# Top-2 gates of a mixture-of-heads layer: both gates in one pass, 16-bit marks, expert outside the head

## The reference

```python
gate_v = jnp.einsum('btc,hec->bthe', x, Ws)      # 16 heads, 8 experts
w, sel = jax.lax.top_k(gate_v, 2)
wsig = jax.nn.sigmoid(w)
oh = jax.nn.one_hot(sel, E, dtype=x.dtype)
mix_v = jnp.einsum('bthk,bthke->bthe', wsig, oh)  # weights of the values
...
gate_o = jnp.einsum('btc,hec->bthe', x, Wd)
_, sel_o = jax.lax.top_k(gate_o, 2)
mask_o = jax.nn.one_hot(sel_o, E, dtype=x.dtype).sum(axis=3)
```

## Time and profile before

| | us |
|---|---|
| median of 3 runs | 2720.51 |
| lowest, highest | 2718.44, 2722.49 |
| profiled execution, its own time | 2725.65 |
| span of the profiled execution | 2723.8 |
| granted TensorE clock, mean | 0.976 of 2.4 GHz |

### The profile page before, as it was taken

One profiled execution on the slowest core, in us unless ns is written; L12 is line 12 of the kernel. 1 busy time (PEld: TensorE's weight loads), 2 busy tenths in 40 slices (PEclk: granted clock), 3 DMA queues, 4 the chain that ended last, 5 costly groups with the idle time before them and its releaser, 6 DMA issues.

```text
span 2723.8 us, 51202 instructions
## 1 busy us (share of the span) xinstructions
PE 2556.2 (94%) x17437; PEld 1698.5 (62%) x17437; DVE 2135.7 (78%) x3151; ACT 1854.0 (68%) x4430; POOL 740.4 (27%) x564
## 2 busy tenths in 40 slices
PE   5699998999999999999899999999999999999997
PEld 3557675665666656566565666656566665666665
DVE  7588776989799798879987998797788879775552
ACT  3366755867688677867767877686687768766663
POOL 1000000544055125504440452264045215400000
PEclk9799999999999999999999999999999999999997
DMA  3425353664566546556573755556466564645434
GB/s 138 139 72 139 94 150 98 162 174 120 150 151 180 129 134 175 139 153 163 133 183 88 198 151 142 162 152 170 111 186 162 148 160 132 189 102 149 113 80 93
DMA packets 753406, 385.77 MB, mean 142 GB/s; under 512 B 421568, under 2 KB 678656, under 8 KB 752768
## 3 DMA queue, kind: packets, MB, share of 16 engines
q1 hardware_dynamic: 747104, 380.66, 52.5%
q10 hardware_dynamic: 6048, 1.84, 0.3%
HBM read 274.91 MB, written 115.87 MB: 143 GB/s over the span
## 4 chain that ended last, share of the span: by engine, by line
PE 65%; DVE 17%; issue 7%; DMA 4%; ACT 3%; SPq 2%; POOL 2%; ACTq 0%; DVEq 0%; POOLq 0%
PE ps L717 14%; PE ps L739 13%; PE ps L726 12%; PE ps L786 7%; PE ps L706 7%; DVE h_ring L1226 5%; PE ps L792 4%; DVE h_nmax L1048 3%; PE ps L799 2%; SPq L515 2%; DVE h_ring L1236 1%; DMA v_d<-h_v_mixed 1%; PE ps L758 1%; POOL h_ring L653 1%; PE ps L826 1%
## 5 line engine op out<-in xcount | busy, mean ns | idle before, releaser
L893 ACT ACTIVATE h_prob<-ps,h_nmax 128x512 f32<-128x512 f32 x1024 | 709.7, 695 | 96.5 <-DVE h_nmax L1048 94.6
L1048 DVE TENSOR_REDUCE h_nmax<-ps 128x2 f32<-128x1024 f32 x512 | 621.6, 1214 | 117.0 <-PE ps L717 116.0
L726 PE MATMUL ps<-ident,h_prob 128*128 128x128 f32 x4096 | 620.8, 279 | 23.4 <-DVE h_probT L1288 13.3
L726 PEld LDWEIGHTS ps<-ident,h_prob 128*128 128x128 f32 x4096 | 479.3, 144 | 193.5 <-issue 115.2
L717 PE MATMUL ps<-h_qk 64*128 64x512 f32 x2048 | 585.5, 649 | 1.4 <-ACT h_prob L893 1.2
L1013 ACT ACTIVATE h_probT<-ps 128x512 f32<-128x512 f32 x796 | 478.0, 600 | 61.7 <-PE ps L726 59.3
L662 POOL TENSOR_TENSOR h_wide_c<-h_wide_c,h_ring 128x512 f32<-128x512 f32 x240 | 333.3, 1389 | 678.6 <-DVE h_ring L1236 678.6
L739 PE MATMUL ps<-h_probT,h_v_sb 128*64 128x256 f32 x4096 | 502.4, 388 | 6.0 <-DMA h_v_sb<-v_d 4.2
L739 PEld LDWEIGHTS ps<-h_probT,h_v_sb 128*64 128x64 f32 x4096 | 273.2, 137 | 312.8 <-issue 149.5
L1226 DVE TENSOR_TENSOR_SCAN h_ring<-h_ring 128x512 f32<-128x512 f32 x256 | 406.5, 1588 | 39.3 <-POOL h_ring L653 24.9
L653 POOL TENSOR_TENSOR h_ring<-h_m_xpad,h_m_b_rows 128x512 f32<-128x512 f32 x256 | 351.0, 1381 | 263.1 <-DVE h_m_xpad L1347 251.5
(11 more groups left out here) (215 smaller groups left out, 2597.7 us busy)
## 6 DMA issues: line engine op xcount, KB each, us to landing
h_mix_diag<-mix_blocks SPq DMA_DIRECT2D x128, 512.0 KB, 4.1
v_d<-h_v_mixed SPq DMA_DIRECT2D x128, 256.0 KB, 4.3
h_v_sb<-v_d SPq DMA_DIRECT2D x128, 256.0 KB, 3.3
at_d<-h_att SPq DMA_DIRECT2D x128, 256.0 KB, 3.1
h_mo_diag<-mo_blocks SPq DMA_DIRECT2D x128, 256.0 KB, 3.5
h_att<-at_d SPq DMA_DIRECT2D x128, 256.0 KB, 3.7
h_m_b_rows<-dbl_d SPq DMA_DIRECT2D x128, 256.0 KB, 4.5
h_m_c_rows<-dbl_d SPq DMA_DIRECT2D x128, 256.0 KB, 4.5
```

Of the source, the lines that this page charges most:

```text
L726: ins = pe.transpose(ps[:, TB + v % 2, k * P:(k + 1) * P], prob[:, v % NB, k * P:(k + 1) * P], ident[:, :])
L893: act.activation(prob[:, v % NB, :], ps[:, SB + v % 4, :], ACT.Exp, bias=nmax[:, p, j, o:o + 1], accum_out=den[:, p, j, o:o + 1]).then_inc ...
L1048: dve.tensor_reduce(nmax[:, p, j, :], ps[:, SB + 2 * w % 4:SB + 2 * w % 4 + 2, :], X, ALU.max, negate=True).then_inc(sem("row_max"), 1)
```

## The change

Both gates go through `top2` together: 12 steps at prep steps 18 to 29, each over 1024 elements per partition (2 gates x 4 rows x 8 experts x 16 heads), and none at steps 45 to 56. The gates are laid out with the expert outside and the head innermost: the weights `gateT` are turned into this order once at the start, when ScalarE copies them from PSUM. So the maximum over experts runs over elements that lie 16 apart, and the mix no longer has to change the order; the marks of the output gate are turned back, in f32, by the last instruction. `key`, `pick`, `first_key` and the maximum of the keys are 16-bit whole numbers; the gates and their maximum stay f32. The first greatest gate is taken away in place in `gates`. The greatest gates lie in the memory of the layer norm's result, which has been turned by then. `mix` and the marks of the output gate have memory of their own, and the wait for the mix's DMA stands before the next job's mix. The last step has two sums of 512 elements, and the mix is one instruction. The store of the marks stays at step 57.

```diff
-        first_key = sb("first_key", [P, E])
+        first_key = sb("first_key", [P, E * H], U16)
...
-            g_top = t("g_top", [P, J * H])
-            g_key = t("g_key", [P, J * H, E])
-            g_rest = t("g_rest", [P, J, H * E])
-            chosen = t("chosen", [P, 2, J, H * E])
-            g_sig = t("g_sig", [P, J, H * E])
-            mix = g_key[:, :, :].rearrange("p (j e a) b -> p j e (a b)", j=J, e=E)
+            GATES_AT_ONCE = 2
+            g_top = nrm[:, 0, 0:GATES_AT_ONCE * J * H].rearrange("p (n h) -> p n h", h=H)
+            g_first = t("g_first", [P, GATES_AT_ONCE * J, H], U16)
+            g_key = t("g_key", [P, 2, J, E * H], U16)
+            g_pick = t("g_pick", [P, 2, J, E * H], U16)
+            chosen_o = t("chosen_o", [P, J, H * E])
+            g_sig = t("g_sig", [P, J, E * H])
+            mix = t("mix", [P, J, E * H])
...
-                                    sp.wait_ge(sem("chosen"), 2 * n + 2)
-                                    sp.dma_start(rows(mo_d[n]), chosen[:, 1, :, :]).then_inc(sem("mo_out"), 16)
+                                    sp.wait_ge(sem("chosen_o"), n + 1)
+                                    sp.dma_start(rows(mo_d[n]), chosen_o[:, :, :]).then_inc(sem("mo_out"), 16)
...
-                                act.wait_ge(sem("chosen"), 2 * n)
+                                act.wait_ge(sem("chosen_o"), n)
...
                     def top2(i, a, m):
+                        n = GATES_AT_ONCE * J
                         r, part = divmod(m, TOP_PARTS)
...
+                        g, key, pick = (z[:, a:a + GATES_AT_ONCE, :, :].rearrange("p a j (e h) -> p (a j) e h", h=H)
+                                        for z in (gates, g_key, g_pick))
+                        top, first = (z[:, :, :].rearrange("p n (o h) -> p n o h", o=1).broadcast_to([P, n, E, H])
+                                      for z in (g_top, g_first))
+                        by_expert = first_key[:, :].rearrange("p (n c) -> p n c", n=1).broadcast_to([P, n, E * H])
                         linked()
+                        if m == TOP_PARTS - 1:
+                            link(dve.scalar_tensor_tensor(
+                                out=g.rearrange("p n e h -> p (n e h)"), in0=pick.rearrange("p n e h -> p (n e h)"),
+                                scalar=NEG, in1=g.rearrange("p n e h -> p (n e h)"), op0=ALU.mult, op1=ALU.add))
+                            return
                         if part == 0:
-                            link(dve.tensor_reduce(g_top[:, :], g, X, ALU.max))
+                            link(dve.tensor_reduce(g_top[:, :, :], g.rearrange("p n e h -> p n h e"), X, ALU.max))
                         elif part == 1:
-                            if a == 1:
-                                dve.wait_ge(sem("mix_out"), 16 * (i + 1))
                             link(dve.tensor_tensor(key, g, top, ALU.is_equal))
                         elif part == 2:
-                            link(dve.tensor_tensor(key, key, fk, ALU.mult))
+                            flat = key.rearrange("p n e h -> p n (e h)")
+                            link(dve.tensor_tensor(flat, flat, by_expert, ALU.mult))
                         elif part == 3:
-                            link(dve.tensor_reduce(g_top[:, :], key, X, ALU.max))
+                            link(dve.tensor_reduce(g_first[:, :, :], key.rearrange("p n e h -> p n h e"), X, ALU.max))
                         elif part == 4:
-                            if r == 0 and a == 1 and i >= 1:
-                                dve.wait_ge(sem("mo_out"), 16 * i)
-                            link(dve.tensor_tensor(pick if r == 0 else key, key, top, ALU.is_equal))
-                        elif r == 1:
-                            dve.tensor_tensor(pick, pick, key, ALU.add).then_inc(sem("chosen"), 1)
+                            link(dve.tensor_tensor(pick if r == 0 else key, key, first, ALU.is_equal))
                         else:
...
+                            if a == 0:
+                                ins = dve.tensor_tensor(g_pick[:, 0, :, :], g_pick[:, 0, :, :], g_key[:, 0, :, :], ALU.add)
+                                ins.then_inc(sem("chosen_v"), 1)
+                            if a + GATES_AT_ONCE == 2:
+                                if i >= 1:
+                                    dve.wait_ge(sem("mo_out"), 16 * i)
+                                dve.tensor_tensor(chosen_o[:, :, :].rearrange("p j (h e) -> p j e h", e=E),
+                                                  g_pick[:, 1, :, :].rearrange("p j (e h) -> p j e h", h=H),
+                                                  g_key[:, 1, :, :].rearrange("p j (e h) -> p j e h", h=H),
+                                                  ALU.add).then_inc(sem("chosen_o"), 1)
...
                     def mix_gates(i):
...
-                        for j in range(J):
-                            ins = dve.scalar_tensor_tensor(out=mix[:, j, :, :].rearrange("p e h -> p h e"),
...
+                        if i >= 1:
+                            dve.wait_ge(sem("mix_out"), 16 * i)
+                        dve.wait_ge(sem("chosen_v"), i + 1)
+                        dve.scalar_tensor_tensor(out=mix[:, :, :], in0=g_sig[:, :, :], scalar=1.0, in1=g_pick[:, 0, :, :],
+                                                 op0=ALU.add, op1=ALU.mult).then_inc(sem("mix"), 1)
...
-                                for a in range(2):
+                                for a in range(0, 2, GATES_AT_ONCE):
                                     if TOP_AT[a] <= u < TOP_AT[a] + 2 * TOP_PARTS:
                                         top2(n, a, u - TOP_AT[a])
```

More of the change, by code:

```diff
@@ L17 @@
 U32 = mybir.dt.uint32
+U16 = mybir.dt.uint16
 ALU = mybir.AluOpType
@@ L414, in macaron_kernel @@
             turns = [(w_raw["L0_W"][:, 0, :], WkT[:, :]), (w_raw["L0_W"][:, 1, :], WvT[:, :])]
-            turns += [(w_raw["Ws"][:, 0, :], gateT[:, 0, :]), (w_raw["Wd"][:, 0, :], gateT[:, 1, :])]
+            turns += [(w_raw[name][:, 0, :], gateT[:, a, :].rearrange("p (e h) -> p e h", h=H)) for a, name in enumerate(("Ws", "Wd"))]
             turns += [(w_raw["Wv"][:, a, :], WveT[:, a * P:(a + 1) * P]) for a in range(E * DH // P)]
@@ L627, in _ @@
                                     sp.dma_start(mix_d.rearrange("(j p) c -> p j c", p=P),
-                                                 mix[:, :, :, :].rearrange("p j e h -> p j (e h)")
+                                                 mix[:, :, :]
                                                  ).then_inc(sem("mix_out"), 16)
@@ L677, in _ @@
                             for e in range(E):
-                                pool.memset(first_key[:, e:e + 1], float(E - e)).then_inc(sem("masks"), 1)
+                                pool.memset(first_key[:, e * H:(e + 1) * H], float(E - e)).then_inc(sem("masks"), 1)
                             for h in range(HALVES):
@@ L994, in _ @@
                         act.wait_ge(sem("w_turned"), n + 1)
-                        act.activation(dst, ps[:, n % 2, 0:D], ACT.Copy).then_inc(sem("w_turned_out"), 1)
+                        src = ps[:, n % 2, 0:D]
+                        if len(dst.shape) == 3:
+                            src = src.rearrange("p (h e) -> p e h", h=H)
+                        act.activation(dst, src, ACT.Copy).then_inc(sem("w_turned_out"), 1)
                     act.wait_ge(sem("w_turned_out"), len(turns))
@@ L1103, in top2 @@
-                        key = g_key[:, :, :]
-                        pick = chosen[:, a, :, :].rearrange("p j (h e) -> p (j h) e", e=E)
-                        linked()
+                        g, key, pick = (z[:, a:a + GATES_AT_ONCE, :, :].rearrange("p a j (e h) -> p (a j) e h", h=H)
+                                        for z in (gates, g_key, g_pick))
+                        top, first = (z[:, :, :].rearrange("p n (o h) -> p n o h", o=1).broadcast_to([P, n, E, H])
+                                      for z in (g_top, g_first))
@@ L1119, in top2 @@
-                            link(dve.tensor_tensor(pick if r == 0 else key, key, top, ALU.is_equal))
-                        elif r == 1:
-                            dve.tensor_tensor(pick, pick, key, ALU.add).then_inc(sem("chosen"), 1)
-                        else:
-                            link(dve.scalar_tensor_tensor(
-                                out=g_rest[:, :, :].rearrange("p j c -> p (j c)"),
-                                in0=pick.rearrange("p n e -> p (n e)"), scalar=NEG,
-                                in1=gates[:, a, :, :].rearrange("p j c -> p (j c)"), op0=ALU.mult, op1=ALU.add))
@@ L1128, in mix_gates @@
-                    def mix_gates(i):
-                        dve.wait_ge(sem("chosen"), 2 * i + 1)
-                        linked()
-                        for j in range(J):
-                            ins = dve.scalar_tensor_tensor(out=mix[:, j, :, :].rearrange("p e h -> p h e"),
```

(8 more changed lines are left out.)

## The result

The changed kernel takes 2796.76 us (median of 4 runs, 2791.96 to 2801.1) against 2719.57: a ratio of 1.0265, 95% interval 1.0245 to 1.0286, so 72 us or 2.6% slower. The forecast was slower, by 28 us. The direction came as predicted and the size at two and a half times, above the upper end of the range.

The account below looks back on a forecast made before the run. No single engine was the bound: TensorE held 65% of the chain, VectorE 17%, full in A with room in B. 39 + 7 - 12 - 4 - 2 = +28 us on 2720.5 gave 2748 us, range 2706 to 2786.

Parts of the forecast that it names:

- A: Prep steps 18 to 30, value gate's top-2 and mix: grows by 6.9 us against 1.8 us idle; 39 us together.
- First job: Its gates run before attention starts and are the chain itself, so all 6.9 us count: 7 us.
- D: A windows of jobs 4, 6, 8 and 14, where VectorE is the chain: all 24 us of surplus count.
- M: A windows of jobs 5, 10 and 11, VectorE a fifth to under half of the chain: 7 of 18 us count.
- P: The other eight A windows, VectorE next to nothing in the chain: a quarter of 34 us counts, 8 us.
- The 1.7 us between a row maximum and its exponential: Seen in A of job 12; a lag of that size was to cost nothing, the rest of 4.3 us per window in part.
- B: Steps 45 to 57, output gate's top-2: shrinks by 8.2 us; gives 12 us in jobs 1, 3, 9 and 4 elsewhere.
- The 2 us for fewer clashes with GpSimd: VectorE's two-input time per job falls from 11.9 to 8.6 us, so fewer clashes: -2 us.
- the stride was not free: Rival on the strided reduces in A: they cost nothing extra, A grows by 3.9 us, about 2725 us; chance 0.18.
- the 16-bit products and compares: Rival on A: 16-bit operations run at full length (1.2 us), A grows by 9.3 us, 2768 us; chance 0.12.
- hardly any lag was absorbed: Against the rival that score banks absorb the lag in A, giving 2708 us, or 2700 with cheap reduces; chance 0.22.
- C: Steps 31 to 44, between the two gate windows; the forecast had no term for it.

Follow-up runs that it names:

- five: Kernel before without the rule for ties, five gate instructions in place of twelve per gate; against the kernel before 0.9875, -34 us.
- the half dose: Kernel before with five added reduces of 512 elements, 3.4 us, in every second of prep steps 19 to 28; against the kernel before 1.0107, +29 us.
- a_plus10: Kernel before with ten added reduces of 512 elements, 6.8 us, one a step in prep steps 19 to 28; against the kernel before 1.0264, +72 us.
- no_b: Kernel before with the output gate's twelve top-2 instructions replaced by one copy of the value gate's marks; against the kernel before 0.9984, -4 us.

## Why the prediction missed the size

1. *Prices of the operations*: right within 0.1 us, but for the 16-bit strided reduce (2.04 for 1.89) and the turned sum (1.28 for 1.02). By the groups' busy time, with what overlap with GpSimd adds, the gates in A went from 9.9 (half of the top-2 groups, and the mix) to 16.9 us a job: 7.0 more, where 6.9 was said.
2. *First job*: 7 forecast, 8 measured, of which 1.3 lie before its gates.
3. *What the extra costs in A*: this is the step that failed. I had the surplus over the idle right, 24 + 18 + 34 = 76 us in D, M and P, and then let it count in full in D alone, four tenths in M and a quarter in P: 39 us. The windows grew by 21.6, 16.5 and 34.8: 73 us. The share of the chain that an engine holds tells what a microsecond less gives, as five shows. For a microsecond more, its idle tells more, and in P VectorE was nearly as full as in D (2.6 us idle a window against 1.0). The 1.7 us between a row maximum and its exponential I had taken as room for a lag in every window; the half dose lengthened A by 24.5 us where its surplus is 31, so such room gave back 6 or 7 us over all fifteen windows at most. One rival is left for a part of it. TensorE's granted clock fell in most of the longer windows, and its busy time in A rose from 461.62 to 476.81 us. In a_plus10 seven A windows stayed at the full clock and grew by 21.8 us for a surplus of 28; the eight at 0.88 to 0.96 grew by 45.9 for 46. So most of the loss comes without the clock, and whether the clock adds some us is open.
4. *B*: 16 forecast, 8 measured (6.4 in no_b): TensorE and SyncE's queue hold it. Of the jobs 1, 3 and 9, which were to give 12, only job 3 gave much (3.4; the others 0.9 and 0.4), and job 2 gave 3.0.
5. *SyncE's wait for the mix* (L627, now L630): it was 12.4 us after 12.5; I had said that it grows. The 2 us for fewer clashes with GpSimd can't be told apart in any run.
6. *Rivals*: the stride was not free, the 16-bit products and compares took 0.68 us and not 1.22, and hardly any lag was absorbed. All three were decided by durations and windows as named. With the surplus counted in full and 8 for B, the same sum is 76 + 7 - 8 - 2 = +73. That this is the measured 73 to the microsecond is partly luck, since steps 0 to 17, the tail and C have no term in it and nearly cancel with what A fell short of its surplus.

## What to carry to other kernels

Where two engines are both full in a stretch, ask for the idle time of the one that you load, not for its share of the chain: here the chain's share told what a reduction gave, the idle what an addition cost, and by busy time the two differed two- to threefold. Moving work out of a stretch with room into a full one costs nearly all of what goes beyond the idle there, even if the total shrinks, so place first and then make it cheaper. Doubling the width of these instructions saved only 0.14 us a pair (1.22 us for 1024 f32 elements against twice 0.68), and a stride in the reduced index took back more than that (0.68 and 0.83 us a reduce).

## What the runs showed of the hardware

- A reduce over an index 16 elements apart: f32 1.89 us and 16-bit 2.04 us for 128x1024, against 1.21 for either when contiguous. That is 0.66 and 0.81 ns more per element. The rule of the Trainium skill (Vector Engine (DVE) Microarchitecture Reference, Measured stream behaviour) of some 0.65 cycle, 0.68 ns, for an element hop agrees for f32 reads. The 2.5 ns that it has for both sources, or the destination alone, at a step of 24 words did not come for a single source at 16; no run here has a step of 24.
- Two-input 16-bit operations took 0.68 us for 1024 elements, with an operand that repeats whole rows too, and 1.21 with an operand that repeats one element. The first is nearly the duration of 512 f32 elements, the second that of 1024. The tier table of the Trainium skill (VectorE: DVE Perf Modes, The perf-mode tier table), by which tensor_tensor on 2-byte operands runs at twice its f32 rate, agrees with the first.
- VectorE's f32 operations with two inputs took longer in the mean when GpSimd had an instruction open beside them, its reduces did not. In the kernel before, the product at L1113 took 0.68 us in 45 instances without such overlap and 0.90 in the mean (at most 1.58) in 19 with it; the scan 1.21 us in 76 and 1.75 in 180; the reduce at L1115 0.68 us either way. After the change 167 scans overlapped and took 1.64 us in the mean, and the 89 others 1.22: that is the fall of the scan's busy time.
- TensorE's granted clock, as the mean of a window, was 0.88 to 0.96 of 2.4 GHz in twelve of the fifteen A windows after the change, as in the job 12 line above, where all but jobs 6 and 8 had been at full. It fell in windows where TensorE had more gaps (busy 31.05 of 34.60 us there). Since VectorE holds most of these windows and no run changes the clock alone, what it cost is not shown.
